# Six orders changed in a one-core kernel of a stencil, an attention pooling, an FC layer and nine experts

## The reference: what is computed

```
x = x + zX*lap_features(x) + zY*lap_tokens(x) + zR*x*(1-x)            # stencil, reflecting edges
s = tanh(x @ W1 + b1) @ v                                             # one score per token
x = x + softmax over l of (s[l] where mask(j, l)) @ x / count(j)      # mask by type: l<=j, l>=j or l!=j
h = gelu(x @ fc1.T + b); x = x + [h @ fc2.T, h @ expert_w[id].T] + b  # FC layer, 1024 hidden
x = x + (1-sg) * sum_e g_e * (silu(x@Wg_e) * (x@Wu_e)) @ Wd_e         # 8 routed experts
      + sg * (silu(x@Sg) * (x@Su)) @ Sd                               # and a shared one, 1024 hidden each
```

## Time and profile before

| | |
|---|---|
| median of 3 runs | 1237.8 us (1236.59 to 1239.88) |
| profiled execution | 1236.2 us |
| its span, first to last instruction | 1234.0 us |
| granted TensorE clock, mean over the span | 1.000 |
| PE busy | 1219.7 us, 99% |
| DVE busy | 871.6 us, 71% |
| ACT busy | 637.4 us, 52% |
| POOL busy | 14.9 us, 1% |

### The profile page before, as it was taken

How to read it: one execution, slowest core, us unless ns; L and a number is a source line. 1 busy time by engine, 2 the same in 40 slices (tenths; PEclk the granted TensorE clock), 3 DMA queues, 4 the chain that set the end, 5 groups by cost and what they waited for, 6 DMA issues and landing times.

```text
span 1234.0 us, 16072 instructions
## 1 busy us (share of the span) xinstructions
PE 1219.7 (99%) x5386; PEld 993.3 (80%) x5386; DVE 871.6 (71%) x1479; ACT 637.4 (52%) x1060; POOL 14.9 (1%) x40
## 2 busy tenths in 40 slices
PE   8999999999999999999999999999999999999998
PEld 4678788888888888888888888888888888888886
DVE  8757686777577767776776687668757875777555
ACT  4655664554455545544554455445545554454443
POOL 4000000000000000000000000000000000000000
PEclk9999999999999999999999999999999999999999
DMA  8311010011001101010101010001000100010000
GB/s 233 61 52 37 28 39 1 26 39 39 1 27 38 38 0 38 25 38 0 38 25 38 0 51 25 25 0 51 25 25 12 51 25 13 13 38 1 17 17 35
DMA packets 20542, 39.75 MB, mean 32 GB/s; under 512 B 7074, under 2 KB 8610, under 8 KB 20386
## 3 DMA queue, kind: packets, MB, share of 16 engines
q1 hardware_dynamic: 19088, 37.30, 9.9%
q0 software_dynamic: 544, 2.10, 0.9%
q10 hardware_dynamic: 882, 0.02, 0.0%
HBM read 37.31 MB, written 2.10 MB: 32 GB/s over the span
## 4 chain that ended last, share of the span: by engine, by line
PE 92%; DVE 5%; ACT 1%; issue 1%; DMA 0%; DVEq 0%; ACTq 0%
PE ps L1089 92%; DVE h_lo L980 1%; DVE w_lo L871 0%; DVE fcw_lo L726 0%; DVE poly L681 0%; ACT poly L426 0%; DVE x_lo L854 0%; DMA sc_in<-in_scalars 0%; ACT stage L553 0%; DVE xT L737 0%; DVE poly L710 0%; DVE x_dn L786 0%; DVE chunk_max L762 0%; ACT h_hi L557 0%; DVE x_dn L757 0%
## 5 line engine op out<-in xcount | busy, mean ns | idle before, releaser
L1089 PE MATMUL ps<-xc_hi,w_hi 128*128 128x512 f32 x1008 | 392.6, 389 | 1.0 <-DVE ps L1009 0.8
L1089 PE MATMUL ps<-xc_lo,w_hi 128*128 128x512 f32 x1008 | 392.2, 389 | 0.0
L1089 PE MATMUL ps<-xc_hi,w_lo 128*128 128x512 f32 x1008 | 392.2, 389 | 0.0
L590 ACT ACTIVATE silu<-ps 128x512 f32<-128x512 f32 x144 | 86.2, 599 | 325.2 <-PE ps L1089 325.2
L1089 PE MATMUL ps<-h_hi,w_hi 128*128 128x512 f32 x576 | 224.4, 390 | 0.9 <-DVE h_lo L995 0.5
L1089 PE MATMUL ps<-h_hi,w_lo 128*128 128x512 f32 x576 | 224.1, 389 | 0.0
L1089 PE MATMUL ps<-h_lo,w_hi 128*128 128x512 f32 x576 | 224.1, 389 | 0.0
L1089 PEld LDWEIGHTS ps<-xc_hi,w_hi 128*128 128x128 f32 x1008 | 189.2, 188 | 42.0 <-DVE ps L1009 1.2
L1089 PEld LDWEIGHTS ps<-xc_hi,w_lo 128*128 128x128 f32 x1008 | 189.2, 188 | 39.4
L1089 PEld LDWEIGHTS ps<-xc_lo,w_hi 128*128 128x128 f32 x1008 | 189.2, 188 | 39.1
L995 DVE TENSOR_TENSOR h_lo<-hidden,h_hi 128x512 fp32r<-128x512 f32 x144 | 99.7, 692 | 145.1 <-ACT h_hi L604 145.1
(11 more groups left out here) (141 smaller groups left out, 1002.6 us busy)
## 6 DMA issues: line engine op xcount, KB each, us to landing
piece<-in_moe_w SPq DMA_DIRECT2D x72, 384.0 KB, 3.1
out_x<-xT SPq DMA_DIRECT2D x8, 256.0 KB, 2.4
xT<-in_x_rows SPq DMA_DIRECT2D x2, 528.0 KB, 5.3
raw<-in_fc_w SPq DMA_DIRECT2D x1, 1024.0 KB, 7.5
x_up<-in_x_rows SPq DMA_DIRECT2D x1, 1024.0 KB, 9.3
x_up<-in_x_rows POOLq DMA_DIRECT2D x1, 1024.0 KB, 9.1
x_nb<-in_x_rows SPq DMA_DIRECT2D x1, 1022.0 KB, 12.4
x_nb<-in_x_rows POOLq DMA_DIRECT2D x1, 1022.0 KB, 10.6
```

The source lines that it names most:

```text
L590: nc.scalar.activation(silu1[:, :], ps[:, BANK_E, :], ACT.Silu).then_inc(silu1_done, 1)
L1089: return nc.tensor.matmul(out_ap, lhsT, rhs, start=first, stop=last, skip_group_check=shared)
```

## The change

Six orders are changed.

1. **Cleared constants.** Five buffers are cleared by DVE ahead of its first work, and no longer by POOL, which waits for them by the semaphore `cleared`. Beside it, DVE does batch 0's second `stencil_tokens` before its first `stencil_square`.
2. **Batch 1's polynomials** go from before `x2_high(0)` on ACT to after the first and second `h_hi` of the FC layer. On DVE, `x2_low(1)` and parts of `fc_low` (the low halves of the FC weights) go to later places.
3. **Score columns.** For batch 1 the scores by token are no longer a PE product with a single column (`score_columns`), but the diagonal of the broadcast scores, taken on DVE (`diagonal`: a multiply with the identity and a reduce per half).
4. **Weight pieces** 1 to 4 of the first expert are prepared at other places of the FC layer's third and fourth block rows.
5. **The first expert group.** Its first products (`group_first`) stand after down block 5 of the last token block, its second (`group_second`) after down block 6; its `gate1_seed` stands ahead of the last FC adds on DVE.
6. **The last group's** down products start with both products of the high part and wait for the low part only then (`down_high_first`).

```diff
+            pool.wait_ge(cleared, 5)
...
             nc.scalar.activation(table_probe[:, :], b1_sb[:, :], ACT.Gelu)
-            stencil_poly(1, 0)
-            stencil_poly(1, 1)
             x2_high(0)
             x2_high(1)
-            between = {(0, 3): [lambda: fc_weights(4, FCW // FCP)],
+            between = {(0, 0): [lambda: stencil_poly(1, 0)],
+                       (0, 1): [lambda: stencil_poly(1, 1)],
+                       (0, 3): [lambda: fc_weights(4, FCW // FCP)],
...
+            nc.vector.memset(blend_src[:, :, :], 0.0).then_inc(cleared, 1)
+            nc.vector.memset(own_chunk[:, :], 0.0).then_inc(cleared, 1)
+            nc.vector.memset(ones[:, :], 1.0).then_inc(cleared, 1)
+            nc.vector.memset(outer_w[:, :, :], 0.0).then_inc(cleared, 1)
+            nc.vector.memset(ctx_parts[:, :, :].bitcast(f32), 0.0).then_inc(cleared, 1)
...
+            def diagonal(h):
+                part = x_nb[:, h, 0:TB].rearrange("p (k l) -> p k l", l=P)
+                link(nc.vector.tensor_tensor(part, scores_of(1, h), wide(ident[:, :], 1, [P, KC // NTB, P]), ALU.mult))
+                link(nc.vector.tensor_reduce(col[:, half(h)], part, AX, ALU.add))
...
-                dve.wait_ge(cols_ps, NTB * (b + 1))
+                if b == 0:
+                    dve.wait_ge(cols_ps, NTB)
+                by_token = ps[:, COL_BANK, 0:KC] if b == 0 else col[:, :]
...
             stencil_tokens(0, 0)
+            stencil_tokens(0, 1)
             stencil_square(0, 0)
-            stencil_tokens(0, 1)
...
             pooled_added(1)
-            fc_low(3, 6)
-            x2_low(1)
-            between = {(0, 0): [lambda: stencil_square(1, 0), lambda: fc_low(6, 8)],
-                       (0, 1): [lambda: stencil_rows(1, 0)],
+            fc_low(3, 5)
+            between = {(0, 0): [lambda: fc_low(5, 6), lambda: stencil_square(1, 0)],
+                       (0, 1): [lambda: fc_low(6, 8), lambda: stencil_rows(1, 0)],
...
-                       (0, 6): [lambda: fc_low(8, 9)],
-                       (0, 7): [lambda: fc_low(9, 10)],
-                       (1, 0): [lambda: masked_scores(1, 0), lambda: maxima(1, 0)],
-                       (1, 1): [lambda: masked_scores(1, 1), lambda: maxima(1, 1), lambda: row_maxima(1)],
+                       (0, 6): [lambda: x2_low(1)],
+                       (0, 7): [lambda: fc_low(8, 10)],
+                       (1, 0): [lambda: masked_scores(1, 0), lambda: maxima(1, 0), lambda: diagonal(0)],
+                       (1, 1): [lambda: masked_scores(1, 1), lambda: maxima(1, 1), lambda: diagonal(1),
+                                lambda: row_maxima(1)],
...
-                     (2, 3): [lambda: piece_low(0, 1), lambda: piece_sums(0, 2)],
-                     (2, 4): [lambda: piece_sums(0, 3)],
-                     (2, 5): [lambda: piece_low(0, 2)],
-                     (2, 6): [lambda: piece_low(0, 3), lambda: piece_sums(0, 4)],
-                     (2, 7): [lambda: token_sums(0, True)],
-                     (3, 0): [lambda: piece_low(0, 4)],
+                     (2, 3): [lambda: piece_sums(0, 2)],
+                     (2, 4): [lambda: piece_low(0, 1)],
+                     (2, 5): [lambda: piece_sums(0, 3)],
+                     (2, 6): [lambda: piece_low(0, 2), lambda: token_sums(0, True)],
+                     (2, 7): [lambda: piece_low(0, 3), lambda: piece_sums(0, 4)],
...
+                if tb == NT - 1:
+                    gate1_seed(0, 0)
                 dve.wait_ge(down_done, RING + FC * (tb + 1))
...
-                       (1, 2): [lambda: score_columns(1, 0), lambda: score_columns(1, 1)],
...
+                        if (tb, k) == (NT - 1, FC - 3):
+                            pe.wait_ge(xlo_done, XT)
+                            pe.wait_ge(x2_summed, NT * DC)
+                            group_first(0, 0)
+                        if (tb, k) == (NT - 1, FC - 2):
+                            group_second(0, 0)
...
+            def down_high_first(e, i, h):
+                k, n = i % FC, e * GROUPS + i
+                high, low = ((h0_hi[:, i % 2, :], h0_lo[:, i % 2, :]), (h1_hi[:, :], h1_lo[:, :]))[h]
+                pe.wait_ge((h0_hi_done, h1_hi_done)[h], n + 1)
+                for c in range(DC):
+                    bank = ps[:, ACC + DC * h + c, :]
+                    mm(bank, w_hi[k][:, D0 - 1 + c, :], high, False, False, True)
+                    mm(bank, w_lo[k][:, D0 - 1 + c, :], high, False, False, True)
+                pe.wait_ge((h0_ready, h1_ready)[h], n + 1)
+                for c in range(DC):
+                    last = mm(ps[:, ACC + DC * h + c, :], w_hi[k][:, D0 - 1 + c, :], low, False, True, True)
+                last.then_inc((down0_done, down1_done)[h], 1)
```

More of the change, by code:

```diff
@@ L122, in stencil_attention_experts @@
         row_max = early("row_max", [P, B, KC])
+        col = early("col", [P, KC])
         exp_in = early("exp_in", [P, B, KC * KC + KC])
@@ L171, in stencil_attention_experts @@
         beside_done = sem("beside_done")
+        cleared = sem("cleared")
         consts_done = sem("consts_done")
@@ L1238, in _, with product, down @@
             ORDER += [("up", FC - 1)] + [("down", k) for k in range(FC - 4, FC)]
+            def product(bank, k, w, p, x, first, last):
+                return split_mm(ps[:, bank, :], ((w_hi[k][:, w - 1, :], w_lo[k][:, w - 1, :]),
+                                                 (xc_hi[p][x][:, :], xc_lo[p][x][:, :])), first, last, True)
+            def down(e, i, h, c):
+                k, p = i % FC, i // FC
+                if k == 0 and not starts(e, i, FC):
+                    pe.wait_ge(acc_read, (e * ROUNDS + p - 1) * NT + DC * (1 - h) + c + 1)
+                if c == 0:
+                    pe.wait_ge((h0_ready, h1_ready)[h], e * GROUPS + i + 1)
+                high, low = ((h0_hi[:, i % 2, :], h0_lo[:, i % 2, :]), (h1_hi[:, :], h1_lo[:, :]))[h]
+                last = split_mm(ps[:, ACC + DC * h + c, :], ((w_hi[k][:, D0 - 1 + c, :], w_lo[k][:, D0 - 1 + c, :]),
+                                                             (high, low)), k == 0, k == FC - 1, True)
+                if c == DC - 1:
+                    last.then_inc((down0_done, down1_done)[h], 1)
@@ new lines, in up0_end, with group_first @@
+            def up0_end(e, i):
+                pe.wait_ge(u1_done, e * GROUPS + i + 1)
+                product(BANK_B + i % 2, i % FC, A22, i // FC, T4, False, True).then_inc(u0_ps, 1)
+            def group_first(e, i):
+                k, p = i % FC, i // FC
+                n = e * GROUPS + i
+                before = not starts(e, i, 1)
+                if p == 0:
+                    pe.wait_ge(wlo_done, e * FC + k + 1)
+                if before:
+                    pe.wait_ge(silu0_done, n)
+                product(BANK_A, k, A11, p, B11, True, False).then_inc(p1_ps, 1)
+                if before:
+                    pe.wait_ge(silu1_done, n)
+                product(BANK_E, k, S1, p, T1, True, False).then_inc(p5_ps, 1)
@@ new lines, in group_second, with group @@
+            def group_second(e, i):
+                k, p = i % FC, i // FC
+                pe.wait_ge(seeded, e * GROUPS + i + 1)
+                product(BANK_A, k, A12, p, B21, False, True).then_inc(g0_ps, 1)
+                product(BANK_B + i % 2, k, S2, p, T2, False, False).then_inc(p6_ps, 1)
+            def group(e, i):
+                k, p = i % FC, i // FC
+                n = e * GROUPS + i
+                before, before2 = not starts(e, i, 1), not starts(e, i, 2)
+                if before:
+                    group_first(e, i)
+                    up0_end(*earlier(e, i, 1))
+                    group_second(e, i)
+                if before2:
+                    down(*earlier(e, i, 2), 0, 1)
+                if before:
+                    down(*earlier(e, i, 1), 1, 0)
+                    down(*earlier(e, i, 1), 1, 1)
+                pe.wait_ge(g1_seeded, n + 1)
+                product(BANK_E, k, S4, p, B22, False, True).then_inc(g1_ps, 1)
+                product(BANK_B + i % 2, k, S3, p, T3, False, False).then_inc(p7_ps, 1)
+                if before:
+                    down(*earlier(e, i, 1), 0, 0)
@@ L1267, in _ @@
                             pooled(1, 1)
-            def product(bank, k, w, p, x, first, last):
-                return split_mm(ps[:, bank, :], ((w_hi[k][:, w - 1, :], w_lo[k][:, w - 1, :]),
-                                                 (xc_hi[p][x][:, :], xc_lo[p][x][:, :])), first, last, True)
-            def down(e, i, h, c):
-                k, p = i % FC, i // FC
-                if k == 0 and not starts(e, i, FC):
-                    pe.wait_ge(acc_read, (e * ROUNDS + p - 1) * NT + DC * (1 - h) + c + 1)
-                if c == 0:
-                    pe.wait_ge((h0_ready, h1_ready)[h], e * GROUPS + i + 1)
-                high, low = ((h0_hi[:, i % 2, :], h0_lo[:, i % 2, :]), (h1_hi[:, :], h1_lo[:, :]))[h]
```

(4 more changed lines are left out.)

84 lines of the change are left out of this document (22 added, 62 removed).

## The result

The changed kernel took 1233.12 us (median of 7 runs, 1231.04 to 1234.25); the kernel before, run beside it on the same chip, 1238.01 us (7 runs, 1236.59 to 1239.88). The ratio is 0.9959, 95% interval [0.9949, 0.9968]: 0.41% less, against a forecast of 1233.2 us. The profiled execution took 1233.12 us with a span of 1231.3 us; that of before was 1236.2 and 1234.0.

What follows compares the result with a forecast made beforehand. PE (TensorE) was taken to bound the kernel, busy 1219.7 of 1234.0 us; 0.25 + 1.05 + 0.7 + 0.4 + 2.1 - 0.4 + 0.45 = 4.55 us off the 1237.8 median gave 1233.2 us, range 1232.0 to 1235.0.

Steps and rivals of the forecast that it cites:

- Step 1: Opening: cleared constants moved to DVE and two DVE steps exchanged let L710 start earlier, gain 0.25 us.
- Step 2: Batch 1's polynomials moved on ACT: PE's first FC matmul comes earlier, gain 1.05 us.
- Step 3: First FC blocks: DVE's xT for batch 1's score layer is ready earlier, gain a further 0.7 us.
- Step 4: Batch 1's score columns: 2.07 us leave PE, but exp waits for DVE's diagonal; only 0.4 us gained.
- Rival D: Before batch 1's outer sums: 2.2 us idle drops PE's clock to 1.2 GHz, kernel slower, 1242.3 us with 40 matmuls; chance 0.05.
- Step 5: Weight pieces in FC's later block rows: PE's waits for a gelu and an h_lo shrink, gain 2.1 us.
- Rival B: Weight pieces: the waits only move and the new order gives nothing, -2.4 us overall, 1235.4 us; chance 0.15.
- Step 6: First group among FC products: 1.25 us of waits go, but PE waits 1.5 us for u_sum; costs 0.4 us.
- Rival A: Passage from FC layer to experts pays in full, DVE's adds not delaying u_sum: -6.2 us overall, 1231.6 us; chance 0.10.
- Step 7: Last group: high products no longer wait for the low half, last adds start earlier, gain 0.45 us.
- Rival C: Opening: POOL's constants late, v_wide at 17, scores 2.4 us later; -2.1 us overall, 1235.7 us; chance 0.08.

Runs made afterwards that it cites:

- open_undo: Changed kernel with the opening's edits undone (five clears on POOL, second neighbours sum behind the square): 1233.34 us, ratio 0.9960 to the kernel before.
- cols: Changed kernel with the score columns' edit alone undone, batch 1's 16 one-column matmuls back on PE: 1231.77 us, ratio 0.9953 to the kernel before.
- after: The changed kernel's own profiled execution, no further edit: 1233.12 us, span 1231.3 us.
- again: The changed kernel once more, unaltered: 1233.1 us, ratio 0.9957 to the kernel before.
- seam_fix: Changed kernel with DVE taking up1_sum and hidden1_mul ahead of piece 5's sums, token sums later, behind FC's last adds: 1233.86 us, ratio 0.9965.
- pieces_undo: Changed kernel with the edit of the weight pieces alone undone, on ACT and DVE: 1233.52 us, ratio 0.9972 to the kernel before.
- seam_undo: Changed kernel with the first expert group's edit alone undone, its first products and seed behind the last FC matmul again: 1232.81 us, ratio 0.9953.
- old: The kernel before once more, unaltered, to profile an execution of its upper level: the profiled one took 1239.97 us.
- warm: Changed kernel with six unused matmuls put into PE's idle time before batch 1's outer sums: 1231.13 us, ratio 0.9945 to the kernel before.

## Why the prediction came out

The number was right, and six of the seven steps, each within 0.15 us. Beside them stood a gain and a loss that no step had, of nearly the same size.

- **Step 1, opening, +0.25: wrong where it was sought.** The second half of xT landed at about 7.4, not 7.1 to 7.2, so DVE waited 0.75 us for it and L711 gained nothing. PE's product took 8.11 us instead of 7.30, which delayed all behind it: PE was free behind the pooled products at 35.24 instead of 34.87. That is the execution's, not the edit's: with the old opening it took 7.96 us too (open_undo). The edit seems to give 0.33 us outside the span, which no step had; that it stands in for the 0.25 is luck.
- **Step 2, polynomials, +1.05: measured 1.04** (from -0.37 to +0.67). **Step 3, +0.7: 0.72.** Undone together: 1.89 in the trace, 2.1 and 1.3 by levels.
- **Step 4, columns, +0.4: 0.46** up to the outer sums (at least 0.25 by cols), with an idle of 1.97 for the 2.2 forecast.
- **Rival D** was priced as a case of its own, at 0.05, a fall that lasts and makes the kernel slower. By the times it happened in 9 of 12 executions, and it cost 1.68 us in the profiled one, since the clock was back at 1.00 by 84 us. Wrong were the chance and the size: the fall ends while PE works on. The levels lie 1.98 us apart, a little more than 1.68, as the profiles with the fall also reach the outer sums a little later (78.56 to 78.93 in after, again, seam_fix and open_undo; 78.43 and 78.55 in pieces_undo and seam_undo).
- **The gain that no step had.** The kernel before lost 1.9 us to a fall of its own in 27 of 37 executions, and the earlier trace rows come from one without. cols and old show such a fall behind the 16 short matmuls that the change takes from PE; that it is this one in most of the 27 is argued, not shown (see old). The changed kernel falls about as often (9 of 12), so by the times the change hardly added a loss: it put one cause, an idle, in the place of another.
- **Step 5, pieces, +2.1: 2.24**, and 2.15 to 2.45 by pieces_undo. Rival B is out.
- **Step 6, seam, -0.4: -0.33.** The wait for u_sum was 1.08, not 1.5. Undone, the edit gives 0.47 back. Rival A is out.
- **Step 7, last group, +0.45: 0.53**, the 2.53 us by which the last adds come earlier less the 2.00 at the last h_hi.
- **Rival C**, constants late: v_wide was there at 11.5 and no wait for it appeared.

The sum of 4.55 was made on an execution without a fall and then taken off a median of executions mostly with one; that it fitted rests on the changed kernel's having one about as often, of another cause and nearly the same cost. That is luck. Level by level the change brings 1236.46 less 1231.3 = 5.2 us and 1238.37 less 1233.28 = 5.1 us. The steps in the span, without the fall and the long product of the profiled execution, are 1.04 + 0.72 + 0.46 + 2.24 - 0.33 + 0.53 = 4.66; 0.08 us go lost again behind the seam, and the 0.33 outside makes 4.9. Without its own fall the changed kernel would have taken 1231.13 us (warm), 2.1 less than forecast.

## What to carry to other kernels

Where executions of one kernel lie at two levels, find out at which the profiled one lies before taking a sum off the median, and look for the stretch with a low clock in a profile of the other level. An idle of 2 us on an engine that is 99% busy costs its own length and, in most executions here (25 of 39), nearly as much again in clock; work without use in the gap paid. When a late value is moved forward in an engine's queue, look at what it overtakes and who waits for that: in seam_fix it was a weight piece, and behind it ACT's next seed.
